# GATv2 attention logits with channels on partitions, contracted on TensorE

## The reference

```python
xl = (x @ Wl + bl).reshape(n, H, C)
xr = (x @ Wr + br).reshape(n, H, C)
e = leaky_relu(xl[src] + xr[dst], 0.2)
logits = einsum('ehc,hc->eh', e, att)
m = segment_max(logits, dst)
p = exp(logits - m[dst])
alpha = p / (segment_sum(p, dst)[dst] + 1e-16)
out = segment_sum(xl[src] * alpha[:, :, None], dst)
x = batchnorm(leaky_relu(out.mean(axis=1) + bias, 0.01) + x)
```

## Time and profile before

| | us |
|---|---|
| median of 3 runs | 9731.46 |
| lowest, highest | 9714.06, 9761.34 |
| span of the profiled execution | 9709.8 |
| TensorE busy in it | 6604.5 |
| VectorE busy | 7234.8 |
| ScalarE busy | 3901.1 |
| GpSimd busy | 5006.8 |

### The profile page before, as it was taken

One profiled execution on the slowest core, in us unless ns is written; L12 is line 12 of the kernel. 1 busy time (PEld: TensorE's weight loads), 2 busy tenths in 40 slices (PEclk: granted clock), 3 DMA queues, 4 the chain that ended last, 5 costly groups with the idle time before them and its releaser, 6 DMA issues. The chain is left out here.

```text
span 9709.8 us, 177827 instructions
## 1 busy us (share of the span) xinstructions
PE 6604.5 (68%) x27124; PEld 4891.7 (50%) x27125; DVE 7234.8 (75%) x15343; ACT 3901.1 (40%) x14623; POOL 5006.8 (52%) x5548
## 2 busy tenths in 40 slices
PE   1677777775577777775577777775466666666666
PEld 0455555544355455544355555554455555555555
DVE  6577777673577677774567677775699999999999
ACT  0244444451144444442144444443144444444443
POOL 2554555421555455530445555540266666666666
PEclk7798899895789899986689889997555555555555
DMA  2111111110111111110111111120000000000000
GB/s 87 30 28 28 28 29 31 27 15 0 30 29 30 27 29 28 31 20 0 26 26 29 28 29 29 28 28 0 22 17 17 17 18 17 17 17 18 17 17 17
DMA packets 219588, 234.03 MB, mean 24 GB/s; under 512 B 74765, under 2 KB 200718, under 8 KB 219150
## 3 DMA queue, kind: packets, MB, share of 16 engines
q1 hardware_dynamic: 95630, 166.18, 5.7%
q0 software_dynamic: 123776, 66.31, 5.4%
HBM read 219.39 MB, written 12.80 MB: 24 GB/s over the span
## 5 line engine op out<-in xcount | busy, mean ns | idle before, releaser
L488 POOL DMA_INDIRECT xg<-table,idx x2880 | 2878.2, 999 | 1239.9 <-issue 818.4
L607 PE MATMUL psum<-wz,xt 128*128 x6072 | 2036.2, 430 | 572.6 <-ACT lin L803 426.7
L622 PE MATMUL psum<-px,oh 128*128 128x272 f32 x5760 | 1738.3, 427 | 379.4 <-issue 192.7
L607 PEld LDWEIGHTS psum<-wz,xt 128*128 128x128 f32 x6072 | 1013.9, 208 | 949.1 <-ACT xt L794 296.2
L622 PEld LDWEIGHTS psum<-px,oh 128*128 128x128 f32 x5760 | 1046.4, 202 | 881.6 <-issue 655.2
L1122 DVE SCALAR_TENSOR_TENSOR u<-psum,atts 128x512 f32<-128x512 f32 x1518 | 1039.9, 685 | 477.8 <-PE psum L609 229.0
L794 ACT COPY xt<-psum 128x256 f32<-128x256 f32 x1440 | 531.2, 369 | 1908.7 <-remote 819.8
L1149 DVE TENSOR_TENSOR px<-xs,pg 128x528 f32 (+1 forms) x1440 | 1010.0, 702 | 315.4 <-issue 238.0
L511 POOL DMA_INDIRECT xg<-table,idx x960 | 931.1, 970 | 582.7 <-issue 148.8
L738 PE MATMUL psum<-w2e,xt 65*128 65x256 f32 x1920 | 1087.0, 670 | 50.7 <-ACT xt L893 45.6
L746 PE MATMUL psum<-acc,oh 128*128 128x32 f32 x1920 | 509.3, 406 | 891.4 <-DVE acc L1480 889.2
(11 more groups left out here) (270 smaller groups left out, 10019.8 us busy)
## 6 DMA issues: line engine op xcount, KB each, us to landing
dr<-dlocs SPq DMA_DIRECT2D x480, 192.0 KB
xg<-table,idx POOLq DMA_INDIRECT x3840
acc<-w_rows SPq DMA_DIRECT2D x160, 192.0 KB
fl<-flags SPq DMA_DIRECT2D x30, 576.2 KB
flags<-fl SPq DMA_DIRECT2D x10, 576.2 KB, 3.2
table<-xn SPq DMA_DIRECT2D x4, 784.0 KB, 3.6
xp<-keys SPq DMA_DIRECT2D x5, 385.0 KB, 4.4
u<-keys SPq DMA_DIRECT2D x5, 385.0 KB, 4.4
```

Of the source, the lines that this page charges most:

```text
L488: nc.gpsimd.indirect_dma_start(out=xg[:, s, t, 96:128], out_offset=None, in_=table, in_offset=bass.IndirectOffsetOnAxis(ap=idx[:, s, t:t + ...
L607: pe.matmul(out_z, xt[:, r, e * P:(e + 1) * P], wz[:, bass.ds(l, 1), :].rearrange("p o z -> p (o z)"), start=True, stop=False)
L622: last = pe.matmul(agg_ps(r), oh[:, r, e, :], px[:, r, e, :], start=(e == 0), stop=(e == 1))
```

## The change

Both z and the logits now have channels, or heads, on partitions.

- z: the layer's weights are the stationary operand (`wnow`, two halves of 128 channels) and `xt` with its 256 edges moves, so z comes out transposed. ACT takes relu(z + bias) into `u` (`rectified`); the bias products of PE go.
- Logits: `contract` multiplies by stationary weights that hold the linear part and 0.8 `att` in just the 8 columns of this step's chunk and zeros elsewhere, and adds up in PSUM over all 48 steps, straight in the layout in which the maxima are scanned. The shifted weights `attc` are windows of an SBUF tile `slide`; SP copies one (3 x 128 columns on 128 partitions, 192 KB) for every three steps. `zero_logits` starts each group's sum with products by zeros. `weighted`, `over_channels`, `chunk_logits` and `linear` go.
- Maxima: ACT copies the sums to `lg` with the constant part as bias; subtraction and exponential come first, in that layout; then PE transposes six tiles, and ACT copies them to `pg`.
- The back's one-hots are made by DVE with two comparisons (`one_hot`) in place of ACT's three operations.
- Bodies have 12 steps, four to a group. There are 12 gather slots, the indices are copied for six steps at once, `oht` has four buffers and `xt` three.
- The table of x is stored after x has been split into three parts, since a wait on `x3_new` is added, and the split is followed by small copies of the layer's weights and biases.
- Self loops: z by the same `zed`; their logits by six matmuls a step with 8 or 4 columns moving, three for each half of its edges, each with `xt` or `u` as the stationary operand (`self_logits`).
- Setup: the weights' loads and foldings change accordingly. The second network's weights `w2e` lie elsewhere and its distance takes a scale of -1.

The core of the diff:

```diff
-S6 = 6
-BODIES = 8
-GS = S6 * BODIES
+SB = 12
+BODIES = 4
+GS = SB * BODIES
...
+                    sp.wait_ge(lgt_done, FRONT0 + l * ZS + k0 + 3 - S6)
+                    sp.dma_start(attc[:, part % 2], slide[:, :, bass.ds(P - H - i * 32 - 8 * part, P)]).then_inc(attl[part % 2], 16)
...
             with sp.Fori(0, LAYERS) as l:
                 sp.wait_ge(x_new, l + 1)
+                sp.wait_ge(x3_new, l + 1)
                 sp.dma_start(table.rearrange("(p b) c -> p b c", p=P), xn[:, 0:BLOCKS, :]).then_inc(tab_new, 16)
...
-                pe.wait_ge(lin_done, AHEAD + l * ZS + n - 1)
+                for half in range(2):
+                    pe.wait_ge(u_done, AHEAD + 2 * (l * ZS + n) - 1 + half)
+                    pe.matmul(zt_ps(half), wnow[:, half], xt[:, s % 3, :], start=True, stop=True).then_inc(z_done, 1)
+
+            def zero_logits(l, g):
+                pe.wait_ge(c_pg, l * GROUPS + g + 1)
+                pe.matmul(lt_ps[:, 0:512], zeros[:], wz[:].rearrange("p l z -> p (l z)")[:, 0:512], start=True, stop=False)
+                pe.matmul(lt_ps[:, 512:CW], zeros[:], wz[:].rearrange("p l z -> p (l z)")[:, 0:CW - 512], start=True, stop=False)
+
+            def contract(l, n, s, t, closes):
+
+                p, j = s // J % 2, s % J
+                pe.wait_ge(attl[p], 16 * t + 16)
+                to = lt_ps[:, j * PAIR:(j + 1) * PAIR]
+                pe.matmul(to, attc[:, p, 2, :], xt[:, s % 3, :], start=False, stop=False)
+                pe.wait_ge(u_done, AHEAD + 2 * (l * ZS + n) + 2)
+                for half in range(2):
+                    last = pe.matmul(to, attc[:, p, half, :], u[:, s % 2, half, :], start=False, stop=(closes and half == 1))
+                last.then_inc(lgt_done, 1)
+
+            def self_logits(l, n, r, s, q):
+
+                pe.wait_ge(l_done, AHEAD + q - 1)
+                pe.wait_ge(u_done, AHEAD + 2 * (l * ZS + n) + 2)
                 for e in range(2):
-                    out_z = z_ps(r)[:, e, :]
-                    pe.matmul(out_z, xt[:, r, e * P:(e + 1) * P], wz[:, bass.ds(l, 1), :].rearrange("p o z -> p (o z)"),
-                              start=True, stop=False)
-                    last = pe.matmul(out_z, ones_b[:], bz[:, bass.ds(l, 1), :].rearrange("p o z -> p (o z)"),
-                                     start=False, stop=True)
-                last.then_inc(z_done, 1)
+                    rows = slice(e * P, (e + 1) * P)
+                    pe.matmul(lg_ps(r)[:, e * H:(e + 1) * H], xt[:, s % 3, rows],
+                              wz[:, bass.ds(l, 1), HC:ZW].rearrange("p o h -> p (o h)"), start=True, stop=False)
+                    for half in range(2):
+                        a = e * H + 4 * half
+                        last = pe.matmul(lg_ps(r)[:, a:a + 4], u[:, r, half, rows],
+                                         attd[:, bass.ds(l, 1), half, :].rearrange("p o h -> p (o h)"),
+                                         start=False, stop=(half == 1))
+                last.then_inc(lgt_done, 1)
...
+                    if a:
+                        contract(l, k0 + s, s, t * 2 + s // S6, ends_group and s >= SB - 2)
                     if b:
                         aggregate(l, g - 1, k0 - GS + s, s)
...
-                pe.wait_ge(l_done, AHEAD + l * QS + (g + 1) * CH)
-                for k in range(2 * J):
-                    last = pe.transpose(lt_ps[:, k * P:(k + 1) * P], lg[:, k].rearrange("p c h -> p (c h)"), ident[:])
-                last.then_inc(c_lt, 1)
...
+                pe.wait_ge(c_p, q + 1)
+                for k in range(2 * J):
+                    last = pe.transpose(lt_ps[:, k * P:(k + 1) * P], lg[:, k].rearrange("p c h -> p (c h)"), ident[:])
+                last.then_inc(c_tpp, 1)
                 pe.wait_ge(c_fd, q + 1)
                 pe.matmul(psum[:, 6, 0:H], fhot[:], fixd[:], start=True, stop=True).then_inc(c_fn, 1)
...
+            def rectified(l, n, r):
+
+                act.wait_ge(lgt_done, FRONT0 + l * ZS + n - 1)
+                for half in range(2):
+                    act.wait_ge(z_done, AHEAD + 2 * (l * ZS + n) + 1 + half)
+                    op.activation(u[:, r, half, :], zt_ps(half), ACT.Relu,
+                                  bias=bnow[:, half:half + 1]).then_inc(u_done, 1)
...
+                act.wait_ge(lgt_done, FRONT0 + l * ZS + (g + 1) * GS)
+                op.activation(lg[:].rearrange("p k c h -> p (k c h)"), lt_ps, ACT.Identity, bias=bnow[:, 2:3]).then_inc(c_lt, 1)
...
-                op.activation(pg[:], lg[:], ACT.Exp).then_inc(c_pg, 1)
+                op.activation(lg[:], lg[:], ACT.Exp).then_inc(c_p, 1)
+                act.wait_ge(c_tpp, q + 1)
+                op.copy(pg[:].rearrange("p k c h -> p (k c h)"), lt_ps).then_inc(c_pg, 1)
...
+            def one_hot(l, k, r):
+
+                v.wait_ge(agg_done, AHEAD + l * NS + k - 1)
+                for e in range(2):
+                    last = op.tensor_scalar(oh[:, r, e, :], iota_f[:], dloc[:, bass.ds(k, 1), e], None, ALU.is_equal)
+                last.then_inc(oh_done, 1)
```

More of the change, by code:

```diff
@@ L166, in gatv2_program, with z_ps, zt_ps, lg_ps @@
         psum = ctx.enter_context(nc.psum_tensor("psum", [P, 8, 512], F32))
-        def z_ps(r, lo=0, hi=ZW):
+        def z_ps(r, lo=0, hi=HC):
             return psum[:, 2 * r:2 * r + 2, lo:hi]
+        def zt_ps(half):
+            return psum[:, 2 + half, 0:PAIR]
+        def lg_ps(r):
+            return psum[:, r, 0:2 * H]
         def xt_ps(r):
@@ L274, in gatv2_program @@
         s_ready = sem("s_ready")
-        gat = [sem(f"gat{s}") for s in range(S6)]
-        drl = [sem(f"drl{h}") for h in range(2)]
+        gat = [sem(f"gat{s}") for s in range(SB)]
+        drl = [sem(f"drl{h}") for h in range(4)]
         front_done = sem("front_done")
@@ L282, in gatv2_program @@
         u_done = sem("u_done")
-        r_done = sem("r_done")
-        lin_done = sem("lin_done")
+        lgt_done = sem("lgt_done")
+        attl = [sem(f"attl{h}") for h in range(2)]
         l_done = sem("l_done")
         oht_done = sem("oht_done")
-        abs_done = sem("abs_done")
-        relu_done = sem("relu_done")
+        oh_done = sem("oh_done")
         px_done = sem("px_done")
@@ L308, in gatv2_program @@
         c_sub = sem("c_sub")
+        c_p = sem("c_p")
+        c_tpp = sem("c_tpp")
         c_pg = sem("c_pg")
@@ L625, in pe_body @@
             def pe_body(l, g, i, a, b, ends_group):
-                k0 = (g * BODIES + i) * S6
+                k0 = (g * BODIES + i) * SB
                 t = (l * GROUPS + g) * BODIES + i
-                for s in range(S6):
-                    if a and (s + 2 < S6 or not ends_group):
-                        front(l, k0 + s + 2, (s + 2) % S6, t + (s + 2) // S6)
-                    if a and (s + 1 < S6 or not ends_group):
-                        zed(l, k0 + s + 1, (s + 1) % 2)
+                for s in range(SB):
+                    if a and (s + 2 < SB or not ends_group):
+                        front(l, k0 + s + 2, (s + 2) % SB, t + (s + 2) // SB)
+                    if a and (s + 1 < SB or not ends_group):
+                        zed(l, k0 + s + 1, s + 1)
+                    if a:
+                        contract(l, k0 + s, s, t * 2 + s // S6, ends_group and s >= SB - 2)
                     if b:
@@ L709, in _ @@
                         self_front(l, i * 2 + 2 + r, r)
+                    for r in range(2):
+                        self_logits(l, NS + i * 2 + r, r, r, l * SELF + i * 2 + r)
                 for r in range(2):
                     zed(l, NS + SELF - 2 + r, r)
+                for r in range(2):
+                    self_logits(l, NS + SELF - 2 + r, r, r, l * SELF + SELF - 2 + r)
                 transposed_sums(l, 0, 0)
@@ L776, in _ @@
             act.wait_ge(s_ready, 2)
-            def one_hot(l, k, r):
-                act.wait_ge(agg_done, AHEAD + l * NS + k - 1)
-                act.wait_ge(relu_done, AHEAD + l * NS + k)
-                for e in range(2):
-                    last = op.activation(dist[:, e, :], iota_f[:], ACT.Abs,
-                                         bias=ndloc[:, bass.ds(k, 1), e])
-                last.then_inc(abs_done, 1)
-                act.wait_ge(abs_done, AHEAD + l * NS + k + 1)
-                op.activation(oh[:, r], dist[:], ACT.Relu, bias=1.0, scale=-1.0).then_inc(relu_done, 1)
@@ L913, in one_hot1 @@
                 for e in range(2):
-                    last = op.activation(dist[:, e, :], iota_f[:], ACT.Abs, bias=ndloc[:, bass.ds(k, 1), e])
+                    last = op.activation(dist[:, e, :], iota_f[:], ACT.Abs, bias=dloc[:, bass.ds(k, 1), e], scale=-1.0)
                 last.then_inc(abs1_done, 1)
@@ L1036, in _ @@
[L1036 to L1041 removed]
+            op.tensor_tensor(bz[:], bz[:], brT, ALU.add)
+            op.scalar_tensor_tensor(attd[:].rearrange("p l a h -> p (l a) h"), attT.unsqueeze(2).to_broadcast([P, LAYERS * 2, 4]), 1.0 - NSLOPE,
```

(7 more changed lines are left out.)

258 lines of the change are left out of this document (117 added, 141 removed).

## The result

The kernel after takes 12,081 us (median of 4 runs, 12,061 to 12,110), beside 9,723 us for the kernel before: ratio 1.243, 95% interval 1.239 to 1.246. Forecast was 10,110, range 9,680 to 10,620. The sign was right; the time is far outside, and past even the 11,160 given for stalls that all stay.

What follows compares the result with a forecast made beforehand. No engine was full; the 27 double groups, with a stall every third step, decided, and PE alone would set their step afterwards. 364 - 45 - 36 + 66 + 32 = +381 on 9,731 gave 10,110 us, range 9,680 to 10,620.

Steps and rivals of the forecast that it cites:

- The stalls: Double groups: PE's waits on late signals and loads, mostly covered after the change, add 3 us a group (0 to +42).
- stalls stay: Rival, double groups: half of 2.63 us per three steps remains on PE, 10,600 us; all of it, 11,160; chance 0.22.
- PE's step: Double groups: PE alone sets the step, 3.52 us when dense, adding 7 us a group (-1 to +9).
- Maxima and restart: Between one double group's steps and the next's: moved transposes, ACT copies and one more hop add 3.5 us a group.
- First groups: Each layer's group with logits alone: POOL's gathers set up to 2.75 us a step, -45 us for three.
- Drains: Each layer's last aggregation: without ACT's one-hots, DVE needs 1.38 us a step; -12 us each, -36 in all.
- Self loops: Self loops of each layer: 6.0 us per two steps instead of 4.3, +66 us in all (0 to +110).
- Start of a layer: Before a layer's first gather: the table's store waits for the split of x, +32 us for three layers.
- Code: Rival: twelve-step loop bodies fetched anew each pass cost 10.7 us a group, 10,400 us; chance 0.07.
- Floor: Rival, double groups: PE's gaps vanish, 3.38 us a step and no stalls, 9,830 us; chance 0.15.
- Faster: Rival: saturated PE stays at 2.4 GHz, 3.37 us a step, 9,570 us, or 9,650 halfway to no change; chance 0.13.

Runs made afterwards that it cites:

- b_run12: The kernel before with twelve gather slots, indices copied for six steps and bodies of twelve steps, its arithmetic kept: 8,426 us, ratio 0.942 to the kernel before.
- before_third: The kernel before, unchanged, run again for its profile on an occasion without late signals: 8,962 us.
- a_pace_again: Second run of the kernel after with indices copied per step, one step ahead, meant for two gathers in a row: 10,012 us, beside 12,258 for the kernel after.
- a_noatt: The kernel after with the shifted attention weights loaded only at the start of a layer, not every three steps: 9,796 us.

## Why the prediction was wrong

**The step that failed** is "The stalls": "I take a quarter of the 12.4, +3 a group; bounds 0 and all of the stalls, 2.63 us per three steps, +42". Measured is +75 a group: 262 us in the kernel after against the 187 that its variants take where no signal is late. (The kernel before took 187 as well, stalls included, so 75 is also the whole difference between the two, where 13.5 was forecast.) The stall was in the trace, and I put it down to the wrong neighbour. SP's load and POOL's run of gathers come once in three steps each, so the trace of before could not tell them apart by their period; the drain, where I looked for a check, has neither. What could have told them apart is behind the earlier trace rows: the run of gathers follows the index copy of 3661.01, its first gather at 3662.23, and the stall ended 8.9 us later, which is the median of the 134 runs of six of that layer that hold signals. Had I listed the late signals against each engine's work, I would have found all of them PE's and all of them inside a run of gathers. And the change altered exactly that: slots from 6 to 12 and the indices for six steps make it twelve in a row. I had counted this as cover ("the gathers twelve"). The rival "stalls stay" had the right place and a bound that took the length of the stall as given. Held from 5 to 17.4 us instead of twice from 5 to 8.9, six steps lose 10 us (30.5 - 20.4) where the kernel before lost 5 against its dense steps. The clock, which falls when PE stands still, had no place in the term.

By occasion, a double group: 162 us for the kernel before and 187 for the kernel after's variants without late signals; 187 to 194 and 262 to 267 with them. So of the 75 us, some 25 are there without late signals too (44 for the arithmetic less 19 for the slots), and 50 are what the longer hold costs beyond what the kernel before already paid (75 against 25).

**The sum, term by term.** PE's step: 3.52 forecast, 3.41 measured; right in kind, and what bounds it fits the profile wherever signals are in time. The comparison, though, was with 3.38, of which 0.9 was more than dense steps take: about half of that goes without late signals (8.9 us for three steps, some 2.9 a step) and the rest with twelve slots (2.5 in b_run12). Against 2.9 it is +0.5 a step, not +0.14.

Maxima and restart: +3.5 forecast, about 0 by subtraction (23.6 against 24). First groups: -15 each forecast, 0 measured (146 and 146) without late signals and +61 to +70 with them. Drains: -12 forecast, +8 measured. The timeline of the drain shows what DVE's step is made of:

```profile
5880.64 1.18 PE L668 MATMUL psum<-px,oh 128*128 128x272 f32 x4 [0.76 <-issue]
5880.77 0.44 DVE L1196 TENSOR_TENSOR acc<-acc,psum 128x272 f32 x1 [0.34 <-issue]
5881.13 0.47 DVE L1170 TENSOR_SCALAR oh<-iota_f,dloc 128x128 f32<-128x128 f32 x2
5881.66 0.71 DVE L1185 TENSOR_TENSOR px<-xs,pg 128x528 f32 x1
...
5882.57 1.18 PE L668 MATMUL psum<-px,oh 128*128 128x272 f32 x4 [0.75 <-issue]
5882.71 0.44 DVE L1196 TENSOR_TENSOR acc<-acc,psum 128x272 f32 x1 [0.34 <-issue]
```

One step is 1.94 us, and DVE sets it. Its sums, one-hots and px take 1.6 us, one behind the other; then it stands 0.34 us ("issue") before the next sums. It doesn't wait for PE there: the product that the sums at 5882.71 add had ended at 5881.82. In between, DVE's sequencer reads the block's number (`value_load`, L1192) and works on up to 5882.66. The kernel before has the same 0.35 us in its drain, with px and the sums alone in a step of 1.59. I had put the work at 1.38 and this at nothing.

Self loops: 6.0 a pair forecast, 6.7 measured (one copy of xt at 5960.86, the next pair's at 5967.57), +30 a layer and +34 up to the last logits (57 to 91 us), not +22. What I had wrong is the clock: the four z matmuls take 3.4 us (5960.68 to 5964.10), not 1.71, at a granted clock of 0.57 from 5960.68 to 5964.40, mostly its 1.2 GHz level, while the twelve small ones take 2.6 and not 3.6. Over the self loops PE is busy 80 of 82 us at a granted clock of 0.75; in before_third it was busy 36 of 52 us at 1.00.

```profile
5960.68 3.63 PE L626 MATMUL psum<-xt,wnow 128*128 128x256 f32 x8
5960.86 0.37 ACT L892 COPY xt<-psum 128x256 f32<-128x256 f32 x1 [0.97 <-PE psum L654]
...
5964.35 0.47 ACT L844 ACTIVATE u<-psum,bnow 128x256 f32<-128x256 f32 x1 [0.38 <-PE psum L626]
...
5967.57 0.37 ACT L892 COPY xt<-psum 128x256 f32<-128x256 f32 x1 [0.97 <-PE psum L654]
```

Start of a layer: +10.5 forecast, +8 and +12 measured from the last logits of the self loops to the first gather, so about right; from the end of the last cast (3245.82) to the first gather (3252.64) it is 6.8 us and not 5.5, of which 5.4 lie behind the issue of the store at 3247.27. Code: no sign of it; the instruction fetches rose from 175 packets to 263, and no run shows that the 3.57 us of the earlier trace rows was a fetch at all.

**The sentences on the Trainium skill.** By the Trainium skill, "TensorE: Matmul & The Clock Gate", section "Back-to-back issue gap", an isolated matmul takes 2.5 ns more than its columns; PE's 3.41 against 3.37 for the columns leaves 0.04 us for 28 passes and all gaps, less than the 0.07 of that rule, so the row's value was the better one. The Trainium skill, "Perfetto Trace Analysis", section "DMA Instruction — HWDGE (DVE, Sync)", says that SyncE and DVE share the block that generates descriptors; no run here shows this to be the cause of anything, since a_pace_again keeps all loads and loses nearly all of the stalls' time.

**Rivals.** "Stalls stay" came nearest, at 11,160 for all of them, still 920 us short. "Floor" (9,830) is, as it turns out, within 0.5% of what the kernel after's variants take without late signals, but by luck: it added 98 to a kernel before of 9,731, and there they lie 825 to 880 above one of 8,947 to 8,978. "Faster" saw PE at its 2.4 GHz level throughout; where that was nearly so (0.94), the kernel after was still 9.5% slower.

**What stays open.** Why a run of gathers holds PE's signals on two occasions and not on four, and by what path. The DMA packets of the gathers start at nearly the same times in both conditions (a twelve-gather run: first at 1.9 to 2.0 us after its first gather, half by 9.4 and 9.7, last at 16.1 and 16.9 us, in the kernel after and in a_noatt), so a slow transfer is not what differs. Whether the length of the run alone slows the kernel before where signals are late, and what the kernel after takes there with six in a row, was not measured. Nor was spacing within a run as a change of its own; but a_pace_again has two stretches of nine gathers that start 1.7 us apart instead of 1.25 to 1.3 (from 4300.7 and 5813.5 us on), and from 3 us into them none of the 13 signals of PE in each is late. That speaks for a limit on how close gathers follow one another, and two stretches are too few to show it.

## What to carry to other kernels

Before counting a stall as covered, find whose signals are late and list everything that has its period; a change that lengthens the one behind it can multiply it. Then ask what the step is without the stall, since on another chip or occasion the stall may be gone. Where a change has two parts, such as slots and arithmetic here, run each alone: one can hide what the other costs. And where work moves to an engine with time to spare, take the engine's whole step from the timeline, with the idle time between its instructions, not the sum of its work.

## What the runs showed of the hardware

- PE's semaphore updates can be held while GpSimd issues indirect DMAs in a row: from 3 to 5 us after the first until 6.0 us (runs of four), 8.9 (six) and 17.4 us (twelve); those of ACT and DVE are not (0.02 us at most), nor is PE's by pairs of gathers. It was so on two of six occasions: the same kernel took 9,723 and 9,904 us there and 8,947 to 8,978 us on the others, where runs of twelve held nothing.
- A step of 28 passes of f32 matmuls (four for each matmul, as the prediction read them from 0.44 us for 264 columns), two transposes and a bf16 product, with all weight loads beside them, took 3.41 us where the prediction had worked out 3.37 us for the columns alone: nearly nothing is lost between them when PE has no wait.
- In the self loops of the kernel after PE was busy 80 of 82 us with a granted clock of 0.75, and four z matmuls took 3.4 us where 0.427 us each at 2.4 GHz make 1.71.
